# A two-layer attention and expert kernel: the setup's second table, the clearing of the slots, and the routing's sums are moved

## The reference

```
xn = layernorm(x);  s = attention0(xn)   # 16 heads of 8, bias that depends on position, softmax
g  = silu(experts(xn))                   # 8 experts, the 2 best of each token, by softmax of xn @ router.T + b
x  = x + s * g
xn = layernorm(x);  s = attention1(xn)   # causal; resid*softmax + skip*I - centre*(mean over the past)
g  = silu(xn @ W.T + b + (xn @ V) @ C.T)
out = x + s * g
```

## Time and profile before

| | us |
|---|---|
| median of 3 runs | 948.13 (947.66 to 950.7) |
| the profiled execution | 952.33 |
| its span, first to last instruction | 950.3 |

### The profile page before, as it was taken

One profiled execution on the slowest core, in us unless ns is written; L12 is line 12 of the kernel. 1 busy time (PEld: TensorE's weight loads), 2 busy tenths in 40 slices (PEclk: granted clock), 3 DMA queues, 4 the chain that ended last, 5 costly groups with the idle time before them and its releaser, 6 DMA issues.

```text
span 950.3 us, 18906 instructions
## 1 busy us (share of the span) xinstructions
PE 794.2 (84%) x6499; PEld 524.4 (55%) x6499; DVE 672.0 (71%) x1142; ACT 478.7 (50%) x851; POOL 269.9 (28%) x302
## 2 busy tenths in 40 slices
PE   1887788888888888876999999155599999999996
PEld 0553455544554544443566666144477777777774
DVE  7637888888888888875677766474465766666672
ACT  1523455555555555544444444277166556565652
POOL 8000755655111111100344444662110101010100
PEclk9977899999999999997999999667699999999999
DMA  5797444434334333304122222421545454545420
GB/s 147 239 195 123 92 96 97 119 96 101 76 81 82 72 67 67 68 14 140 46 68 69 65 68 60 114 80 40 111 91 110 107 109 100 115 100 118 96 62 14
DMA packets 105536, 88.31 MB, mean 93 GB/s; under 512 B 12565, under 2 KB 97497, under 8 KB 102409
## 3 DMA queue, kind: packets, MB, share of 16 engines
q1 hardware_dynamic: 96780, 76.54, 36.3%
q0 software_dynamic: 4352, 8.99, 3.2%
q10 hardware_dynamic: 4352, 2.10, 0.9%
HBM read 45.69 MB, written 41.11 MB: 91 GB/s over the span
## 4 chain that ended last, share of the span: by engine, by line
PE 39%; DMA 6%; ACT 3%; DVE 2%; POOL 1%; issue 1%; SPq 1%; ACTq 0%; POOLq 0%; DVEq 0%
PE ps L763 7%; PE ps L1549 4%; DMA ks<-parts_d 3%; PE ps L784 3%; PE ps L1499 3%; PE ps L1525 3%; PE ps L775 2%; PE ps L765 2%; PE ps L1523 2%; PE ps L1497 1%; ACT rows L979 1%; DMA parts_d<-qk 1%; PE ps L1530 1%; PE ps L1528 1%; PE ps L1504 1%
## 5 line engine op out<-in xcount | busy, mean ns | idle before, releaser
L1270 DVE TENSOR_REDUCE mx<-ps 128x4 f32<-128x1024 f32 (+1 forms) x224 | 268.2, 1217 | 133.4 <-PE ps L1499 79.4
L1404 ACT ACTIVATE probs<-probs 128x1024 f32<-128x1024 f32 x128 | 135.1, 1057 | 143.5 <-DVE probs L1280 141.0
L1280 DVE TENSOR_TENSOR probs<-ps,tabB 128x1024 f32<-128x1024 f32 x128 | 152.3, 1210 | 5.9 <-PE ps L1519 5.9
L1409 ACT ACTIVATE probs<-ps 128x1024 f32<-128x1024 f32 x96 | 96.4, 1023 | 82.3 <-PE ps L1525 59.6
L1549 PE MATMUL ps<-probs,vpad 128*32 128x256 f32 (+1 forms) x2048 | 125.1, 363 | 14.7 <-ACT probs L1404 14.7
L1491 PE MATMUL ps<-tabA,eyeb 128*128 128x512 bf16 x256 | 100.6, 393 | 21.8 <-DVE probs L1280 14.0
L1220 POOL TENSOR_TENSOR qkr<-qkf,qk 128x512 f32<-128x512 f32 x32 | 37.0, 1158 | 255.3 <-ACT qk L1376 255.3
L1493 PE MATMUL ps<-ks,qs 96*128 96x256 bf16 x512 | 100.9, 279 | 0.0
L851 POOL DMA_INDIRECT mixed<-probs x72 | 69.0, 958 | 112.2 <-DVE probs L840 111.5
L1519 PE MATMUL ps<-qs,ks 99*128 99x256 bf16 x512 | 77.3, 281 | 15.3 <-DVE mx L1270 11.3
L1549 PEld LDWEIGHTS ps<-probs,vpad 128*32 128x32 f32 x2048 | 51.8, 109 | 62.7 <-ACT probs L1404 30.7
(11 more groups left out here) (229 smaller groups left out, 1454.9 us busy)
## 6 DMA issues: line engine op xcount, KB each, us to landing
parts_d<-qk SPq DMA_DIRECT2D x64, 192.0 KB, 2.3
qs<-parts_d SPq DMA_DIRECT2D x32, 384.0 KB, 5.0
ks<-parts_d SPq DMA_DIRECT2D x32, 384.0 KB, 6.7
parts_d<-qk SPq DMA_DIRECT2D x64, 128.0 KB, 1.9
slots_in<-cum SPq DMA_DIRECT2D x1, 4680.0 KB, 30.3
probs<-slots_in SPq DMA_DIRECT2D x72, 65.0 KB, 1.8
parts_d<-qk SPq DMA_DIRECT2D x64, 64.0 KB, 1.6
probs<-mixed SPq DMA_DIRECT2D x16, 256.0 KB, 3.4
```

What stands on the lines that cost most here:

```text
L1270: nc.vector.tensor_reduce(mx[:, s.buf(), t, heads[0]:heads[-1] + 1], ring[:, slot].rearrange("p (h n) -> p h n", n=w), AX.X, ALU.max).then ...
L1280: nc.vector.tensor_tensor(probs[:, j, :].rearrange("p (h n) -> p h n", n=T), ring[:, slot].rearrange("p (h n) -> p h n", n=T), v.tabB[:, h ...
L1404: nc.scalar.activation(probs[:, j, :], probs[:, j, :], ACT.Exp).then_inc(exp_done, 1)
L1409: nc.scalar.activation(probs[:, j, :], ring[:, slot], ACT.Exp).then_inc(exp_done, 1)
```

## The change

Setup: the load of tabB is issued behind the stores and loads of the first stacks. The products for the second layer's bias columns, feff and bo (L598 to L607) go ahead of and into the flips of tabA, and VectorE's copies of them forward too. The router's and bias's semaphores are merged (one count more). A ones tile replaces the one built in fw's place.

Clearing: the zeros are a part of `squares` (inside probs), written by GpSimd after the layer norm's second half has read it; the transfer is issued by SP in step 0, after the second stacks, in six pieces a partition, each of 1560 numbers in a row. VectorE waits for it, with the shares' load, at the start of step 1, as probs is then written.

Routing: its scratch is x's own place, which is loaded again by SP at tile 16 of the experts. VectorE keeps the choice (`choose`), in step 0, and in step 2 the tiles' counts and the shares (`tile_counts`, `shares`). PE counts in step 1 at position 6, into misc; ACT copies the counts out and takes the exponentials in step 1 at position 8. GpSimd forms the sums over tiles by five rounds of shifted additions (`place_one`, step 1, ahead of the maxima's parts), the places (`place_two`, step 2, behind them) and the owners (step 10). The scatters start in step 3 in place of step 0, and ten a step run until step 9.

```diff
+    PIECES = 6
+    zeros = v.squares.rearrange("p t d -> p (t d)")[:, 0:SLOT_TILES * (D + 2) // PIECES]
     ZEROED = 10
...
+    def tile_counts(dve):
+        run, more = runs[1][:, PAD:PAD + NT, :], more_sum.rearrange("p (e t) -> p e t", e=E)
+        dve.wait_ge(summed, 1)
+        nc.vector.tensor_tensor(more, run[:, NT - 1, :].unsqueeze(2).broadcast_to([P, E, NT]),
+                                cst[:, C_TILES:C_TILES + NT].unsqueeze(1).broadcast_to([P, E, NT]), ALU.is_gt).then_inc(ended, 1)
+        dve.wait_ge(ended, 1)
+        nc.vector.tensor_reduce(tiles, more, AX.X, ALU.add).then_inc(ended, 1)
+        dve.wait_ge(ended, 2)
+        nc.vector.tensor_tensor_scan(ends, v.onesf[:, 0:E], tiles, 0.0, ALU.mult, ALU.add).then_inc(ended, 1)
+        dve.wait_ge(ended, 3)
+        nc.vector.scalar_tensor_tensor(first_slot, ends, 1.0, tiles, ALU.mult, ALU.subtract).then_inc(ended, 1)
+    def shares(dve):
+        dve.wait_ge(tally_out, 4)
+        nc.vector.tensor_reduce(m2, ew, AX.X, ALU.add).then_inc(shared, 1)
+        dve.wait_ge(shared, 1)
+        nc.vector.reciprocal(v.wt[:, 0, :], m2).then_inc(shared, 1)
+        dve.wait_ge(shared, 2)
+        nc.vector.tensor_tensor(v.wt[:, 1, :], v.wt[:, 0, :], gap, ALU.mult).then_inc(shared, 1)
...
+    def place_one(pool):
...
+        for run in runs:
+            step(nc.gpsimd.memset(run[:, 0:PAD, :], 0.0))
+        pool.wait_ge(tally_out, 2)
+        step(nc.gpsimd.tensor_tensor(runs[0][:, PAD + 1:PAD + NT, :], all_tiles[:, 1:NT, :], all_tiles[:, 0:NT - 1, :], ALU.add))
+        step(nc.gpsimd.tensor_copy(runs[0][:, PAD:PAD + 1, :], all_tiles[:, 0:1, :]))
+        for n, k in enumerate((2, 4, 8, 16)):
+            to, of = runs[(n + 1) % 2], runs[n % 2]
+            add = nc.gpsimd.tensor_tensor(to[:, PAD:PAD + NT, :], of[:, PAD:PAD + NT, :], of[:, PAD - k:PAD + NT - k, :], ALU.add)
+            step(add)
+        step(nc.gpsimd.tensor_copy(runs[1][:, PAD:PAD + NT, :], runs[0][:, PAD:PAD + NT, :]))
+        nc.gpsimd.tensor_tensor(runs[0][:, PAD:PAD + NT, :], runs[0][:, PAD:PAD + NT, :], all_tiles, ALU.subtract).then_inc(summed, 1)
...
+    def place_two(pool):
...
+        def total(m, src):
+            step(nc.gpsimd.tensor_tensor(tree[:, :, 0:4], src[:, :, 0:4], src[:, :, 4:8], ALU.add))
+            step(nc.gpsimd.tensor_tensor(tree[:, :, 4:6], tree[:, :, 0:2], tree[:, :, 2:4], ALU.add))
+            step(nc.gpsimd.tensor_tensor(m.unsqueeze(2), tree[:, :, 4:5], tree[:, :, 5:6], ALU.add))
+        run = runs[0][:, PAD:PAD + NT, :]
+        pool.wait_ge(summed, 1)
+        step(nc.gpsimd.tensor_tensor(run, run, own_tile, ALU.add))
+        pool.wait_ge(ended, 4)
+        step(nc.gpsimd.tensor_scalar(first_slot, first_slot, float(P), None, ALU.mult))
+        step(nc.gpsimd.tensor_tensor(run, run, first_slot.unsqueeze(1).broadcast_to([P, NT, E]), ALU.add))
         for k, hot in enumerate((one1, one2)):
-            step(nc.vector.tensor_tensor(cand, hot, run, ALU.mult))
-            step(nc.vector.tensor_reduce(m1, cand, AX.X, ALU.add))
-            step(nc.vector.tensor_copy(v.place[:, k, :], m1))
-            step(nc.vector.tensor_scalar(v.rowid[:, k, :], cst[:, C_ROWS:C_SPARE], float(k * B * T), None, ALU.add))
-        own = one1.rearrange("p t e -> p (t e)")[0:1, 0:SLOT_TILES]
-        step(nc.vector.tensor_scalar(own, cst[0:1, C_TILES + NT:C_ROWS], ends[0:1, 0:1], None, ALU.is_ge))
+            step(nc.gpsimd.tensor_tensor(cand, hot, run, ALU.mult))
+            total(m1, cand)
+            step(nc.gpsimd.tensor_copy(v.place[:, k, :], m1))
+            step(nc.gpsimd.tensor_scalar(v.rowid[:, k, :], cst[:, C_ROWS:C_SPARE], float(k * B * T), None, ALU.add))
+        pool.wait_ge(shared, 3)
...
+    def owners(pool):
...
+        own, more = more_sum[0:1, 0:SLOT_TILES], more_sum[0:1, SLOT_TILES:2 * SLOT_TILES]
+        step(nc.gpsimd.tensor_scalar(own, cst[0:1, C_TILES + NT:C_ROWS], ends[0:1, 0:1], None, ALU.is_ge))
...
-        for i, src in enumerate((v.bias_r, v.bias_f)):
-            sp.dma_start((v.tabA, v.tabB)[i][:], bass.AP(src, 1, [[1, P], [REL, H], [1, TAB]])).then_inc(tab_ld[i], 16)
+        def table(i, of):
+            sp.dma_start((v.tabA, v.tabB)[i][:], bass.AP(of, 1, [[1, P], [REL, H], [1, TAB]])).then_inc(tab_ld[i], 16)
+        table(0, v.bias_r)
         sp.wait_ge(zeroed, ZEROED)
         first_stacks()
-        sp.wait_ge(bias_mm, 2)
+        table(1, v.bias_f)
+        sp.wait_ge(bias_mm, 3)
         sp.dma_start(braw[0:4 * E, :], v.gu_b.rearrange("e (j n) -> (e j) n", n=P)).then_inc(eb_load, 16)
         sp.dma_start(braw[4 * E:5 * E, :], v.down_b[:, :]).then_inc(eb_load, 16)
         sp.dma_start(braw[5 * E:BIASES, :], v.f_b.rearrange("(a n) -> a n", a=1)).then_inc(eb_load, 16)
-        sp.wait_ge(eb_parts, 1)
-        sp.dma_start(v.slots_in[:, :].rearrange("(t p) d -> p t d", p=P),
-                     v.zero.unsqueeze(1).broadcast_to([P, SLOT_TILES, D + 2])).then_inc(cleared, 16)
         sp.wait_ge(c_load, 16 * 3)
         sp.dma_start(v.share, v.consts[0, C_UT:C_UT + T].partition_broadcast(P)).then_inc(cleared, 16)
+    def sync_clear(sp):
+        sp.wait_ge(zeroed, ZEROED + 1)
+        sp.dma_start(v.slots_in[:, :].rearrange("(p k t) d -> p k (t d)", p=P, k=PIECES),
+                     zeros.unsqueeze(1).broadcast_to([P, PIECES, SLOT_TILES * (D + 2) // PIECES])).then_inc(cleared, 16)
...
+    def gpsimd_clear(pool):
+        pool.wait_ge(ln, layernorm_ready(4) - 2)
+        nc.gpsimd.memset(zeros, 0.0).then_inc(zeroed, 1)
...
-        for n in range(max(first, 0), min(first + count, TOPK * NT)):
+        for n in range(first if first >= 0 else TOPK * NT, min(first + count, TOPK * NT)):
...
         head_order(rowsp, rows, (3, 4))
+        dve.wait_ge(small_mm, 2)
+        nc.vector.tensor_scalar(v.cols[:, 3:4], ps[:, 2, 3:4], QSCALE, None, ALU.mult).then_inc(small_cp, 1)
+        nc.vector.tensor_copy(v.cols[:, 4:5], ps[:, 2, 4:5]).then_inc(small_cp, 1)
+        nc.vector.tensor_copy(fvT, ps[0:RANK, 2, 128:256]).then_inc(small_cp, 1)
+        nc.vector.tensor_copy(fcT, ps[0:RANK, 2, 256:384]).then_inc(small_cp, 1)
         layernorm_scale(nc, dve, v, ln, sq, rs, 1)
...
+    def scalar_late(act, misc):
+        act.wait_ge(counted, 1)
+        nc.scalar.activation(own_tile.rearrange("p t e -> p (t e)"), misc[:, 0:NT * E], ACT.Copy).then_inc(tally_out, 1)
+        nc.scalar.activation(all_tiles.rearrange("p t e -> p (t e)"), misc[:, NT * E:2 * NT * E], ACT.Copy).then_inc(tally_out, 1)
         act.wait_ge(chosen, 3)
-        ew, gap = rt[:, 6], small[:, 3 * NT:4 * NT]
-        nc.scalar.activation(ew, ew, ACT.Exp).then_inc(ex, 1)
-        nc.scalar.activation(gap, gap, ACT.Exp).then_inc(ex, 1)
+        nc.scalar.activation(ew, ew, ACT.Exp).then_inc(tally_out, 1)
...
+        pe.wait_ge(copied, EARLY + 4)
+        for k in range(3, 5):
+            nc.tensor.matmul(ps[:, 2, k:k + 1], rowsp[:, k, :], v.ones[0:1, 0:1], start=True, stop=True)
+        pe.wait_ge(small_cp, 2)
+        nc.tensor.matmul(ps[0:RANK, 2, 128:256], fv, eye, start=True, stop=True)
+        nc.tensor.matmul(ps[0:RANK, 2, 256:384], fc, eye, start=True, stop=True).then_inc(small_mm, 1)
         pe.wait_ge(tab_ld[0], 16)
-        pe.wait_ge(bias_cp, 2)
+        pe.wait_ge(bias_cp, 3)
         for n in range(NB):
+            if n == NB // 2:
+                pe.wait_ge(small_cp, 7)
+                nc.tensor.matmul(ps[:, 2, 0:P], bvb, v.wo0[:], start=True, stop=False)
+                nc.tensor.matmul(ps[:, 2, 0:P], v.ones[0:1, 0:P], bor, start=False, stop=True)
+                nc.tensor.matmul(ps[:, 2, P:2 * P], fw, eye, start=True, stop=False)
+                nc.tensor.matmul(ps[:, 2, P:2 * P], fvT, fcT, start=False, stop=True).then_inc(small_mm, 1)
...
+        hits = both.rearrange("p t e -> p (t e)")
+        nc.tensor.matmul(misc[:, 0:NT * E], cst[:, C_BEFORE:C_BEFORE + P], hits, start=True, stop=True)
+        nc.tensor.matmul(misc[:, NT * E:2 * NT * E], onesf, hits, start=True, stop=True).then_inc(counted, 1)
...
+            if s.k == 16:
+                sp.wait_ge(v.labelled, 2 * TOPK + 1)
+                for half in range(2):
+                    sp.dma_start(v.x[:, 16 * half:16 * half + 16, :],
+                                 v.x_in[8 * half:8 * half + 8].rearrange("b (c p) d -> p (b c) d", p=P)).then_inc(v.x_again, 16)
...
-                if layer == 0 and s.k == 1:
-                    v.sync_late(sp)
                 if s.has(1):
                     stacks(s)
+                if layer == 0 and s.k == 0:
+                    v.sync_clear(sp)
+                    v.sync_late(sp)
...
+                v.gpsimd_clear(pool)
                 for k in range(B):
                     s = Step(k, 0, 3, B)
                     body(s)
-                    v.scatter(pool, 2 * SCATTERS * k - SCATTERS, SCATTERS)
+                    v.gpsimd_late(pool, k)
+                    v.scatter(pool, 2 * SCATTERS * (k - 3), SCATTERS)
```

(31 more changed lines are left out.)

123 lines of the change are left out of this document (51 added, 72 removed).

## The result

The changed kernel takes 943.85 us (median; 941.55 to 950.48) beside 950.64 us for the kernel before in the same series (946.75 to 953.29): a ratio of 0.9935, interval 0.992 to 0.9949, so 6.8 us less. In a second series it was 943.67 us, ratio 0.9943 (0.9921 to 0.9964). The sign was forecast, the size was not: 16.9 us were expected, and 943.85 lies just outside the range. The base has moved too: the forecast was taken off 948.13, a median of three runs, and the twenty of this series have 950.64, so 2.5 us of the 12.7 between 931.2 and 943.85 are the base's. The execution profiled for the first series took 950.48 us (span 948.7); that of the second has a span of 937.6.

The account below looks back on a forecast made before the run. Layer 0 was taken as bound by VectorE's nearly gapless chain, so an earlier step 1 moves everything behind it. Terms -17.06, -3.2, +0.6, +2.3 and +0.5 gave -16.9 us off 948.13: 931.2, range 927.5 to 943.

Parts of the forecast that it names:

- S: Start of step 1 on VectorE in layer 0, put at 79.0 for 96.06, 17.1 us earlier.
- part one: Setup: tabB loaded behind the first stacks, small products earlier; step 0 starts at 48.5, 4.9 us earlier than 53.44.
- The clearing: Clearing of the slots behind the second stacks, in long runs: issued at 61.8, taking 15.7 us, for 30.3 before.
- The rival that the setup isn't shorter: Flips, layer norm and small products hinder each other; step 0 starts at 53.4 as now: -11.9 us, 936.2; chance 0.13.
- that of a clearing as long as before: Clearing still takes 30.3 us, so step 1 starts at 93.1: -2.8 us, 945.3; chance 0.10.
- x loaded again: Reload of x among the experts' tiles, 7.7 us against about 7 us of lead: +0.5 us, bounds 0 and 5.
- a rival priced it at +4.5 us: GpSimd's sums cost +3.5 us and x's reload stalls PE among the experts, +4.5 us: 939.2; chance 0.12.
- GpSimd's sums: Prefix sums in step 1, 0.68 us per operation, 5.5 us in all; they delay the maxima's parts by 0.6 us.
- VectorE in step 2: Four instructions for tile counts and three for shares come back in step 2, where VectorE has no gap: +2.3 us.
- The moving of PE's tally: PE's two tally products go into step 1, where PE waits for VectorE: 0 us.
- Step 2's start: With GpSimd free in step 1, ks is ready for PE and VectorE's two gaps at step 2 shrink: -3.2 us.
- The scatters' move: GpSimd's scatters move from steps 0 to 6 into 3 to 9, long before they are read: 0 us.

Follow-up runs that it names:

- x in step 15: Changed kernel with x loaded again in step 15 of layer 0, ahead of that step's maxima rows, instead of among the experts' tiles: 936.83 us, ratio 0.9856.

## Why the prediction was wrong

By stages, in us, each from two traces of either kernel where nothing else is said:

| stretch | forecast | measured |
|---|---|---|
| start of VectorE's step 1 | -17.1 | -17.1 |
| to the first maximum of step 2 | -1.2 | -0.6 |
| to the first maximum of step 3 | +0.9 | +4.0 |
| rest of layer 0 | 0 | +0.1 |
| experts, first to last gate result | +0.5 | +6.3 |
| sum | -16.9 | -7.3 |

The first row is the mean over six executions that have the changed setup, clearing and waits (82.59, 77.29, 81.63, 77.98, 77.50 and 77.84: 79.14) against the mean of 96.06 and 96.44. The sum stands beside the 6.8 and 6.2 us of the two series, but no closer than a few microseconds: by the two traces alone the first row would be -16.3, and the time behind the last gate result, which the table leaves out, is 2.0 us longer in the changed kernel's two traces. Of the 9.6 us that the sum is short of the forecast, the experts make 5.8 and step 2 to step 3 makes 3.1.

**The setup, right; S in part by luck.** Step 0 starts at 48.3 on average for the forecast 48.5, PE's own setup being the limit, as part one has it. tabB lands at 54.4 to 55.6 for the forecast 54, and hides less well than forecast: in two of the nine executions its products wait for it, by 0.27 and 0.54 us. The choice is done 27.8 to 30.0 us after the start. The clearing was put about 3 us too short: it went by the rate at which the tables are read, whose runs are 1536 bytes for tabB alone (768 for tabA, in bf16), and it is a write. The wait for it is 1.7 to 2.0 us, not 0.6. That S comes out at 79.1 for 79.0 all the same is luck: in the six executions the clearing is issued at 60.2 on average and not at 61.8, and VectorE starts 0.3 us behind its landing, where the forecast had 1 us for the biases' store and half a microsecond of margin. The rival that the setup isn't shorter and that of a clearing as long as before are both out. The second of these would have been true with the old runs.

**x loaded again, the step that failed most.** The mechanism stood in the text (the next tile's load behind 2 MB), and a rival priced it at +4.5 us over the 0.5 taken. It cost 6.3, above the forecast's upper bound of 5. The 0.5 set 7.7 us for the 2 MB against about 7 us of lead. The lead was right (6.8 us from the issue to PE's stop), the 7.7 were misread: in the earlier trace rows they are the median of two halves, each from its own issue, and by the trace the whole took 10.2 us there (from 0.8 to 11.0) and 10.1 among the experts, with the next tile behind it. So PE stood for 3.68 us, and then paid again, because it came back at the lower clock. The text counted the stall and not the clock; how the other 2.6 us divide between the clock and the tiles' pipeline was not measured. The other half of that rival was wrong: GpSimd's sums of 128x256 take 0.71 to 0.79 us each (forecast 0.68), and step 2's parts are not late for PE, which at 101.17 waits for ACT and turns the parts right behind it.

**VectorE in step 2, the second that failed.** Seven instructions were costed by their own length, 2.3 us. They cost 4.6 to 4.8, by the count that GpSimd slows, the stop of PE that they cause and the clock behind it. The moving of PE's tally was costed at nothing, because PE waits for VectorE in step 1; it does, but three positions earlier in the order, and 0.5 and 1.4 us were lost in its two traces.

**Step 2's start, part right.** The gaps closed to 0.74 and 1.79 us, as forecast. The gain from it was 3.2 us against the one trace and 1.1 against the other.

**The scatters' move, put at nothing.** The prediction moved them from steps 0 to 6 into 3 to 9 at no cost, as they are read much later. In four of the ten traces that have them there, the move costs 1.9 to 3.4 us; the two of the changed kernel itself are not among the four. The last section has the rows.

What stays open: the time from the last gate result to the end of the span, nearly all of it layer 1, is 351.6 to 357.1 us in these traces, for either kernel, and no experiment was made on that. With the late start of step 0 it is why a single trace (950.48 here) can stand 6.6 us over its kernel's median. What makes PE's clock rise earlier in one execution's setup than in another's was not tried either.

## What to carry to other kernels

A long transfer put into the queue that feeds a stage without slack costs at least its whole landing time less the lead (10.1 less 6.8 us here), however low the stage's average share of the DMA engines is (0.23 in the earlier trace rows): cut it up, or issue it a stage earlier. A median over several transfers is not the landing time of all of them together. An instruction added to an engine costs its length only where its follower has slack; where PE follows and stops, its lower clock comes on top, and in a gap nearby the same instructions cost nothing. A wait for a whole series of transfers belongs behind the work that others wait for, not ahead of it. A gap seen in one trace should be priced from a second one before it is counted as a gain.

## What the runs showed of the hardware

PE's clock in the setup differs between executions of the same program: the same sixteen logit products take 2.06 us in one and 3.42 in another, step 0's first product 0.38 or 0.59. Step 0 starts at 46.7 to 50.7 us, where no transfer ends later than PE.

A write of 4680 KB to HBM takes 18.2 to 18.9 us in runs of 6240 bytes and 29.1 us in runs of 520, at the same place in the same queue.

VectorE's 128x256 operation with two inputs (L319) takes 1.35 us beside GpSimd's 128x512 operation and 0.41 with GpSimd idle; the 1.35 came out alike in all eight traces that had the two side by side at this place, the 0.41 in both that didn't.

The scatters' landing times differ between executions. GpSimd takes the second 32 of the 64 scatters only when all of the first 32 have landed (L491). In the kernel before this wait stands behind the maxima's parts of step 3, is 1.38 us in both traces, and PE doesn't wait:

```profile
163.16 0.24 POOL L425 COPY rows<-rowid 128x32 f32<-128x32 f32 x1 [1.38 <-DMA slots_in<-rows,place]
```

Started in step 3, the scatters reach it in step 6, ahead of the parts. In six of the ten traces it takes 2.8 to 3.3 us there and nothing is late. In the four others it takes 5.2 to 5.5 us, and PE waits 1.75 to 2.10 us with the turn of the parts, as in the execution with x in step 15:

```profile
206.66 0.24 POOL L494 COPY rows<-rowid 128x32 f32<-128x32 f32 x1 [5.50 <-DMA slots_in<-rows,place]
...
210.86 0.27 POOL L1327 TENSOR_TENSOR m<-mx,nothing 128x32 bf16<-128x32 f32 x1
```

```profile
212.16 0.26 PE L1745 MATMUL ps<-eyeb,m 128*96 128x128 bf16 x1 [2.10 <-POOL m L1333]
```

Steps 6 and 7 are 1.9 to 3.4 us longer in these four. So the change brought this risk: the wait stood behind the parts and now stands ahead of them. What makes the landing longer, and whether a start at another step avoids it, was not tried.
